# Last layer of a four-layer model on one core: inner layer norms in two instructions per tile, residual and bias added by TensorE, last row sum by DMA, expert weights from unnormalised exponentials

## What is computed

```python
# s branch, per sequence (256 channels, 16 states, scan over time)
state = exp(d_t[..., None] * A) * state + (d_t * u_t)[..., None] * b_t[:, None, :]
y_t = einsum('bdn,bn->bd', state, c_t)          # sum over the 16 states
y = (ys + x * D) * silu(z);  out = einsum('bld,ed->ble', y, out_proj_w)

# z branch
attn_out = ao @ Wo + bo                          # 16 heads of 8
x1 = _layernorm(x + attn_out, g1, be1)           # first inner norm
gate_probs = softmax(x1 @ Wg + bg)
topk_p, topk_i = top_k(gate_probs, 2)
topk_p = topk_p / sum(topk_p)                    # two expert weights
comb = sum(one_hot(topk_i, 8) * topk_p[..., None])
y = einsum('bsef,efd->bsed', gelu(einsum('bsd,edf->bsef', x1, W1) + b1), W2) + b2
return _layernorm(x1 + einsum('bse,bsed->bsd', comb, y), g2, be2)   # second inner norm
```

## Time and profile before

| | before |
|---|---|
| runs | 3441.11, 3442.25, 3444.41 us, median 3442.25 us |
| the profiled execution | 3439.86 us, its span 3438.1 us |
| busy over the span | PE 83%, PEld 67%, DVE 71%, ACT 52%, POOL 9% |
| mean granted TensorE clock | 0.857 of 2.4 GHz |
| the last layer's steps | from about 2050 us to the end of the span |

### The profile page before, as it was taken

How to read it: one execution, slowest core, us unless ns; L and a number is a source line. 1 busy time by engine, 2 the same in 40 slices (tenths; PEclk the granted TensorE clock), 3 DMA queues, 4 the chain that set the end, 5 groups by cost and what they waited for, 6 DMA issues and landing times. The chain is left out here.

```text
span 3438.1 us, 59682 instructions
## 1 busy us (share of the span) xinstructions
PE 2858.1 (83%) x19918; PEld 2312.8 (67%) x19918; DVE 2427.4 (71%) x6656; ACT 1779.8 (52%) x4064; POOL 311.1 (9%) x340
## 2 busy tenths in 40 slices
PE   2888888888999989898765568888888888888887
PEld 1777777777888878787654536666666666666665
DVE  3666666656666666666675268888888888888887
ACT  1333333335555555555454346666666666666664
POOL 0000000000000000000022211111111111111111
PEclk9999999999999999999887757777777777777777
DMA  6000000000000000000200223333333333333334
GB/s 189 0 0 0 0 0 0 0 1 0 0 0 0 0 0 0 0 0 0 65 13 25 56 62 83 93 92 92 93 93 93 94 93 93 93 94 93 93 93 105
DMA packets 86467, 163.18 MB, mean 47 GB/s; under 512 B 18856, under 2 KB 45617, under 8 KB 86321
## 3 DMA queue, kind: packets, MB, share of 16 engines
q0 software_dynamic: 20480, 62.93, 9.6%
q1 hardware_dynamic: 64640, 98.15, 8.8%
q10 hardware_dynamic: 1200, 0.27, 0.1%
HBM read 92.60 MB, written 9.99 MB: 30 GB/s over the span
## 5 line engine op out<-in xcount | busy, mean ns | idle before, releaser
L964 ACT ACTIVATE b_neg<-b_neg,b_nmax 128x128 f32<-128x128 f32 (+1 forms) x512 | 228.4, 447 | 272.4 <-DVE b_nmax L1072 271.1
L2492 DVE TENSOR_TENSOR_SCAN d_state<-w,d_state 128x1024 f32<-128x1024 f32 x128 | 291.0, 2284 | 3.8 <-issue 2.4
L2229 ACT ACTIVATE d_probs<-l_bank,w_b 128x256 f32<-128x256 f32 x512 | 210.2, 468 | 156.2 <-PE l_bank L2069 153.6
L2069 PE MATMUL l_bank<-xnT,w_w 128*128 128x256 f32 x1024 | 245.1, 382 | 14.5 <-ACT d_probs L2229 14.5
L1060 DVE SCALAR_TENSOR_TENSOR b_gated<-b_th,l_bank 128x256 f32<-128x256 f32 x256 | 107.5, 420 | 209.7 <-ACT b_th L958 205.5
L2080 PEld LDWEIGHTS l_bank<-w_w,d_probs 128*128 128x128 f32 x2048 | 244.9, 192 | 11.7 <-ACT d_probs L2229 5.3
L2080 PE MATMUL l_bank<-w_w,d_probs 128*128 128x128 f32 x2048 | 252.7, 276 | 0.0
L96 POOL TENSOR_TENSOR ln_rstd<-ln_var_eps,minus_half 128x2 f32<-128x2 f32 x51 | 64.6, 1266 | 1858.0 <-DVE ln_var_eps L90 1858.0
L1999 PE MATMUL l_bank<-w 9*128 9x256 f32 x1040 | 205.8, 669 | 25.1 <-ACT w L2154 18.9
L2191 ACT ACTIVATE w<-d_delta,d_negA 128x255 f32<-128x255 f32 x520 | 220.1, 498 | 0.0
L2069 PEld LDWEIGHTS l_bank<-xnT,w_w 128*128 128x128 f32 x1024 | 184.7, 190 | 41.1 <-ACT d_probs L2229 21.3
(11 more groups left out here) (405 smaller groups left out, 6983.7 us busy)
## 6 DMA issues: line engine op xcount, KB each, us to landing
d_bct<-l_bc SPq DMA_DIRECT2D x132, 512.0 KB, 3.9
d_state<-d_state POOLq DMA_DIRECT2D x96, 512.0 KB, 6.6
d_state<-d_state POOLq DMA_DIRECT2D x32, 256.0 KB, 4.2
x_sorted<-x SPq DMA_DIRECT2D x1, 2560.0 KB, 16.3
w<-in_L_ffn_w_dram SPq DMA_DIRECT2D x1, 2048.0 KB, 10.1
w_w<-in_L_ffn_W_dram SPq DMA_DIRECT2D x1, 2048.0 KB
c2e_xg<-x_sorted SPq DMA_DIRECT2D x16, 128.0 KB
y_sorted<-c2e_yo SPq DMA_DIRECT2D x16, 128.0 KB, 1.8
```

What stands on the lines that cost most here:

```text
L964: done = nc.scalar.activation(neg[:, h % RP, cols], neg[:, h % RP, cols], ACT.Exp, bias=nmax[:, h % RP, a:a + 1], scale=-1.0, accum_out=to ...
L2069: done = nc.tensor.matmul(bank[:, b, i * T:(i + 1) * T], w.w1[:, e, k * P:(k + 1) * P], x1T[:, :], start=True, stop=True)
L2229: done = v.activation(hid[:, e % 2, k, :], bank[:, b, i * T:(i + 1) * T], ACT.Gelu, bias=w.b1[:, e, k:k + 1])
L2492: done = v.tensor_tensor_scan(group, dA[i][:, g % (NG - 1), :, :].rearrange("p m t -> p (m t)"), group, 0.0, ALU.mult, ALU.add)
```

## The change

It has five edits in `layer3`, here with the names that the diff uses.

1. Residual and output bias: POOL's `residual` goes. PE adds them in PSUM: a product of the identity with the 256 columns of `xn` (two tiles side by side), one with the broadcast bias, and then the two output projections into the same place. DVE's addition of `resid` goes too, and the first inner norm reads PSUM.
2. Both inner norms: instead of (x - mean) * rstd, then * weight, then + bias (two instructions, then one wide, then one wide), each tile takes `inner_shift`, (x - mean) * weight, which doesn't need rstd, and later `inner_scale`, * rstd + bias. `inner_shift` stands right behind the statistics, `inner_scale` where the application stood.
3. The last two state rows are added by one more DMA pair on POOL's queue, which waits for the pair before it. DVE's addition (L2597) goes.
4. The router takes the best two of the unnormalised exponentials (their sum, its reciprocal and the product with it go), since the two weights are divided by their own sum anyway.
5. The cast of the indices moves between the sum of the two and its reciprocal.

```diff
@@ tensor: behind the q/k/v rows of tile 0
                     pe.wait_ge(xnT_ready, n + 2)
                     qkv_rows(0)
+                    attended = bank[:, 5, 0:TILES * D].rearrange("p (a d) -> p a d", d=D)
+                    nc.tensor.matmul(attended, c.ident[:, :], xn[:, par, :, :], start=True, stop=False)
+                    nc.tensor.matmul(attended, c.ident[:, :], wide_bo, start=False, stop=False)
                     pe.wait_ge(y_ready, n + 1)
...
                         done = nc.tensor.matmul(bank[:, 5, a * D:(a + 1) * D], yT[:, a * P:(a + 1) * P], w.o[:, :],
-                                                start=True, stop=True)
+                                                start=False, stop=a == TILES - 1)
@@ gpsimd
-                    residual(n + 1, 1 - par)
...
                     for i in range(CI):
-                        pool.dma_start(st[i][:, 0:2, :], st[i][:, 2:SG, :], accum_op=ALU.add).then_inc(sum_ready, 16)
+                        pool.dma_start(st[i][:, 0:2, :], st[i][:, 2:SG, :], accum_op=ALU.add).then_inc(pair_added, 16)
                     inner_power(2 * n + 2)
+                    pool.wait_ge(pair_added, 16 * CI * (n + 1))
+                    pool.sem_inc(pool_step, 1)
+                    for i in range(CI):
+                        pool.dma_start(st[i][:, 0, :], st[i][:, 1, :], accum_op=ALU.add).then_inc(sum_ready, 16)
@@ vector
-            def inner_apply(out, weight, bias, count):
...
+            def inner_shift(out, src, weight):
+                for a in range(TILES):
+                    v.scalar_tensor_tensor(out=out[:, a, :], in0=src[:, a, :], scalar=meanvar[:, a, 0:1],
+                                           in1=weight[:, :], op0=ALU.subtract, op1=ALU.mult)
+
+            def inner_scale(out, bias, count):
+                v.drain()
                 dve.wait_ge(rstd_ready, count)
                 for a in range(TILES):
...
+                    done = v.scalar_tensor_tensor(out=out[:, a, :], in0=out[:, a, :], scalar=rstd[:, a:a + 1],
+                                                  in1=bias[:, :], op0=ALU.mult, op1=ALU.add)
+                return done
...
                     dve.wait_ge(o_in_psum, n + 1)
-                    dve.wait_ge(resid_ready, n + 1)
-                    v.tensor_tensor(rows[:, :, :], bank[:, 5, 0:TILES * D].rearrange("p (a d) -> p a d", d=D),
-                                    resid[:, :, :], ALU.add).then_inc(rows_ready, 1)
-                    v.drain()
-                    inner_stats()
+                    attended = bank[:, 5, 0:TILES * D].rearrange("p (a d) -> p a d", d=D)
+                    inner_stats(attended)
+                    inner_shift(x1, attended, w.g1)
                     take_qkv(n + 1, 0)
-                    inner_apply(x1[:, :, :], w.g1, w.be1, 2 * n + 1).then_inc(x1_ready, 1)
+                    inner_scale(x1, w.be1, 2 * n + 1).then_inc(x1_ready, 1)
...
-                    inner_stats()
+                    inner_stats(rows)
+                    inner_shift(rows, rows, w.g2)
                     second_part(n + 1)
                     for blk in range(NBLK):
                         heads_max(n + 1, blk)
                     third_part(n + 1, 1 - par)
-                    inner_apply(rows[:, :, :], w.g2, w.be2, 2 * n + 2).then_inc(gate_ready, 1)
+                    inner_scale(rows, w.be2, 2 * n + 2).then_inc(gate_ready, 1)
...
-                    v.drain()
-                    for i in range(CI):
-                        v.tensor_tensor(ym[:, i, :], ym[:, i, :], st[i][:, 1, :], ALU.add)
```

More of the change, by code:

```diff
@@ L1832, in layer3 @@
         yT = c.xnT
-        resid = c.xn
         x1 = sb("x1", [P, TILES, D])
@@ L1857, in layer3 @@
         xnT_ready = sem("xnT_ready")
-        resid_ready = sem("resid_ready")
         qkv_in_psum = sem("qkv_in_psum")
@@ L1877, in layer3 @@
         o_in_psum = sem("o_in_psum")
-        rows_ready = sem("rows_ready")
         var_ready = sem("var_ready")
@@ L1913, in layer3 @@
         pool_step = sem("pool_step")
+        pair_added = sem("pair_added")
+        route_step = sem("route_step")
         sum_ready = sem("sum_ready")
@@ L1925, in _ @@
             wqkv = w.qkv[:, :, :].rearrange("p i d -> p (i d)")
+            wide_bo = w.bo[:, :].unsqueeze(1).to_broadcast([P, TILES, D])
             def turn_x(m, par):
@@ L2270, in _ @@
         def _(pool):
[L2271 to L2276, removed]
             def inner_power(count):
@@ L2284, in _ @@
             norm_power(nc, c, s, 0)
-            residual(0, 0)
             with pool.Fori(0, NSEQ // 4) as m:
@@ L2351, in _ @@
             v.memset(qk[:, :, 1, :, HD3:QK], 1.0)
-            dve.sem_inc(rows_ready, 1)
             dve.sem_inc(acc_taken, 2)
@@ L2436, in third_part, with inner_stats @@
                 v.tensor_tensor(du[:, :, :], delta[:, :, :], xs[:, par, :, :], ALU.mult)
-            def inner_stats():
+            def inner_stats(src):
                 for a in range(TILES):
-                    v.bn_stats(stats[:, a, :], rows[:, a, :])
+                    v.bn_stats(stats[:, a, :], src[:, a, :])
                 v.drain()
@@ L2445, in inner_stats @@
                 v.tensor_scalar(var_eps[:, :], meanvar[:, :, 1], LN_EPS, None, ALU.add).then_inc(var_ready, 1)
-            def inner_apply(out, weight, bias, count):
+            def inner_shift(out, src, weight):
[4 more added lines that the diff above has]
+                v.drain()
                 dve.wait_ge(rstd_ready, count)
                 for a in range(TILES):
-                    v.tensor_scalar(rows[:, a, :], rows[:, a, :], meanvar[:, a, 0:1], rstd[:, a:a + 1],
-                                    ALU.subtract, ALU.mult)
-                v.drain()
-                wide = [x[:, :].unsqueeze(1).to_broadcast([P, TILES, D]) for x in (weight, bias)]
-                v.tensor_tensor(rows[:, :, :], rows[:, :, :], wide[0], ALU.mult)
-                v.drain()
-                return v.tensor_tensor(out, rows[:, :, :], wide[1], ALU.add)
+                    done = v.scalar_tensor_tensor(out=out[:, a, :], in0=out[:, a, :], scalar=rstd[:, a:a + 1],
+                                                  in1=bias[:, :], op0=ALU.mult, op1=ALU.add)
+                return done
             def heads_max(n, blk):
@@ L2546, in _ @@
                     scan(2, 0)
-                    route_best(nc, r, n)
+                    v.wait_ge(r.exped, n + 1)
+                    v.sem_inc(route_step, 1)
+                    for a in range(TILES):
+                        v.max(r.best[:, a, :], r.logits[:, a, :])
+                    v.drain()
+                    for a in range(TILES):
+                        v.max_index(r.index[:, a, :], r.best[:, a, :], r.logits[:, a, :])
                     v.tensor_tensor(psum2[:, :], r.best[:, :, 0], r.best[:, :, 1], ALU.add)
                     v.drain()
+                    v.tensor_copy(r.place[:, :, :], r.index[:, :, :])
                     v.reciprocal(psum2[:, :], psum2[:, :])
```

## The result

The changed kernel takes 3451.39 us (median of 8 runs, 3448.94 to 3454.26), the kernel before 3442.02 us (8 runs, 3438.80 to 3444.41). The ratio is 1.0028, 95% interval 1.0017 to 1.0039: slower by 9.4 us, where 3453 had been forecast against 3442.25. The profiled execution took 3454.01 us, its span 3452.3 us.

A forecast was written before the change was run, and what follows sets the result against it. PE was taken to bound B, DVE to bound C and the four maxima behind it, with DVE idle time in A. B +7.2, C +7.4 and A -3 gave +11.6 us, so 3453 us; own range 3447 to 3461, overall 3436 to 3468.

The forecast's parts named there:

- The identity products: On PE behind L1934, in B: nothing hides them, +1.0 us per step, bounds 0.86 and 1.73.
- B: Stretch from the turned outputs to the end of expert 7, bounded by PE: +0.45 us per step, 7.2 in all.
- The logits: In B: state_input ends earlier, so DVE takes the router logits at once, saving up to 0.55 us per step.
- The second norm in C: inner_shift put ahead of the first maximum: 0.55 us, 0.09 absorbed by waits, so +0.46 per step.
- C: Stretch from the last expert to the first maximum, bounded by DVE: +0.46 us per step, 7.4 in all.
- ym: In A: ym comes 1.7 us sooner, PE uses only what it waits: -3 us in all, bounds 0 and -4.
- The signs in the profile: New DVE waits for output projection (0.7 us) and logits (about 1), longer ones at s_out and turned outputs, longer C.
- A: Stretch from the last maximum to the turned outputs, some 30 us, where DVE has idle time: -3 us in all.
- DVE's time: Rival: DVE's work is what counts, 3.5 us less per step, 56 in all, 3386 us; chance 0.14 for 3386 to 3435.
- a hole for the products: Rival: the identity products fit into PE's hole before L2102 and cost nearly nothing, 3440 us; chance 0.16.
- scores that hide the half of the norm: Rival: the scores hide the new pair in C, so C is 0, sum +4 us, 3446; chance 0.08.
- the products run wholly at the low level: Rival: identity products run at 1.2 GHz throughout, B 1.18 us per step, +26 us in all, 3468; chance 0.10.

The follow-up runs named there:

- e4: Changed kernel, but VectorE again adds the last state row (no second DMA pair) and the router normalises before taking the best two: 3449.44 us.
- e1: Changed kernel without the identity products: residual and bias again by GpSimd, with one addition on VectorE; 3436.54 us.
- f4: Kernel before, with only the first inner norm split into inner_shift behind the statistics and inner_scale in place of the application: 3434.49 us.
- f3: Changed kernel with the pair of identity products done twice at the same place: 3479.15 us.
- e2: Changed kernel with the second inner norm's inner_shift moved behind the maxima: 3448.78 us.
- e3: Changed kernel without identity products and with the second inner norm's inner_shift behind the maxima: 3428.38 us.
- g1: Kernel before plus two identity products with unused results, in PE's gaps ahead of and behind the last heads_out: 3435.07 us.
- g3: Changed kernel with its products around the last heads_out and second inner_shift behind the maxima, plus an unused product ahead of each of the first three heads_out: 3427.11 us.
- f1: Changed kernel with its two identity products moved into PE's gaps, one ahead of the last heads_out and one behind it: 3423.45 us.

## Why the prediction was right, point by point

*The bound.* That DVE's saved time would become waits was right, and e4 and e1 show it.

*The identity products.* Forecast 1.0 us per step, between 0.86 and 1.73 (at 2.4 and at 1.2 GHz). Measured 1.70 and 0.86 for the pair in the two steps shown, and 1.04 per step as their effect on B (changed against e1). Right: the pair itself takes 1.37 us in the mean, and the work behind it gives 0.3 of that back, as forecast. The spread was wider than thought: B lasts 41.9 to 43.2 us per step in the changed kernel, 41.8 to 42.3 before.

*The logits.* Forecast 0.55 us per step; 7.9/16 = 0.49 in B between the kernel before and e1, of which 0.10 lies ahead of x1's transposes and is not theirs; 0.41 in f4. So about 0.4. x1 itself gave nothing, as forecast: it waits two us for PE.

*B in all:* 8.8 us against 7.2, mainly because the logits gave less.

*The second norm in C.* 6.8 us against 7.4, but made up otherwise, and the nearness is in part luck. The prediction read that DVE works from 2536.70 to 2541.16 without a gap and is the bound of C. It was not quite: in the kernel before DVE stood still for 0.12 to 0.34 us before the first maximum in all 16 steps, 2.6 us in all, where the wait view books only 1.4, and the scores came last. So in steps without a stall the 0.52 us of `inner_shift` (2372.06 to 2372.58) lengthened C by only 0.31, from 4.46 to 4.77: most of the rest fell into that idle time, and the maximum now starts 0.08 us before the end of its predecessor (2374.13 + 0.69). What made up for it were stalls of 0.45 us that landed in C in four steps, 1.8 us in all, which the prediction had not seen.

*ym.* 5.2 us against 3: `ym` had been late by more than the booked 1.8 us, in every step (39.64 to 39.47 in the ordinary ones, 40.00 to 39.47 in every fourth).

*Router and DMA pair.* Nothing, as forecast; the last sum lands some 8 us ahead of its reader.

*The signs in the profile.* The waits for the projection (0.9 us against 0.7) and for the logits (1.1 against 1) came, and the one for s_out grew by 1.7 (1.5). The one at the reciprocals was forecast to grow too, and it shrank, from 39.4 to 32.5 us. Here the prediction was wrong, in a place that its sum does not use: DVE takes up its chain at the copy of s_out, which had not moved (it ends 19.63 us behind the first maximum in both kernels), while the turned outputs came earlier by what A gained, 5.2 us; most of the rest is a stall that grew in every fourth step (2.64 us of wait there before, 1.73 now). "The waits of A shrink" was also named as a sign of being wrong: one of the two did, but both together grew from 52.6 to 73.4 us.

Sum: 8.8 + 6.8 - 5.2 = 10.4 us in the stretches, 9.4 in the medians, 11.6 forecast. Three mechanisms were right; that the sum is nearer than its terms is luck, since B came out 1.6 us above its forecast and A 2.2 below. The rivals fell: DVE's time (e1, e4), a hole for the products (f3), scores that hide the half of the norm (e2, e3; they hid 0.2 of its 0.52 us). That the products run wholly at the low level came true in six of the 16 steps only. What the prediction did not see at all is that the same products a few us earlier would pay by the clock.

## What to carry to other kernels

An engine with a high share may still wait once per step for the same partner. Then work taken from it buys nothing, while work added to the partner costs in full. So before work is moved off an engine, look where it waits, and whether the engine that takes the work is idle at the new place. If an edit splits an operation so that a part of it can go early, put that part into idle time and not ahead of what the others wait for; moving two pieces turned +9 us into -19 here. And a PE gap ahead of a dense stretch can be worth filling: in this kernel two added products in such gaps brought the clock's rise forward and saved 7.3 us (g1). More of them is not better by itself (g3).

## What the runs showed of the hardware that was not expected

TensorE's granted clock stays at 0.50 (1.2 GHz) in the attention stretch although PE's matmul row is full there. The window of the kernel before:

```profile
2655.00:2660.00 5.00, 5.00 (x30) 2.48 (x32) 4.66 (x4) 5.00 (x11) 0.00 (x0) 0.50 0.00 2
```

Those are products over 9 rows and into 32 columns of the array (L1999 and L2057). Two products over all 128 rows, in two gaps, were followed by the 2.4 GHz level earlier in all 16 steps, in a kernel that needed them (f1) and in one that didn't (g1): 7.3 us of 3442 for work that nobody uses. Whether it counted that they use all rows of the array or that they filled gaps, no run tells apart.

A busy row is thus no sign of the clock. Two rows of one line can differ by a factor of two, 1.70 and 0.86 us for the same pair in one run.

And DVE has stalls of its own of about 0.4 us in every fourth step, at an instruction that changes with the code: in C in the changed kernel, in the routing in e4. With that place C changed by 2.3 us. What causes them no run shows.
